# Writes of the routed rows moved from SyncE's DMA queue to ScalarE's, with four buffers in place of two

## The reference

```
scores  = sigmoid(xf @ router_w.T)                  # 4096 rows, 16 experts
4 experts per row, picked within the 2 best of 4 groups; w = their scores, made to sum to 1
shared  = silu(xf @ shared_gate.T) * (xf @ shared_up.T) @ shared_down.T
routed  = sum over a row's 4 experts e of  w[e] * (silu(xf @ gate[e]) * (xf @ up[e])) @ down[e]
out     = x + shared + routed
```

## Time and profile before

| | |
|---|---|
| time, three runs | 1189.49 us median (1186.09, 1189.49, 1204.87) |
| profiled execution | span 1205.0 us; no time of its own is given beside it |
| busy: TensorE matmul / weight load | 87% / 50% |
| busy: VectorE, ScalarE, GpSimd | 53%, 32%, 37% |
| block stage in the profiled execution | about 556 to 954 us |
| last stage | about 954 to 1205 us |

### The profile page before, as it was taken

How to read it: one execution, slowest core, us unless ns; L and a number is a source line. 1 busy time by engine, 2 the same in 40 slices (tenths; PEclk the granted TensorE clock), 3 DMA queues, 4 the chain that set the end, 5 groups by cost and what they waited for, 6 DMA issues and landing times.

```text
span 1205.0 us, 22651 instructions
## 1 busy us (share of the span) xinstructions
PE 1046.4 (87%) x6496; PEld 603.5 (50%) x6497; DVE 638.2 (53%) x1454; ACT 386.1 (32%) x751; POOL 444.0 (37%) x517
## 2 busy tenths in 40 slices
PE   7899499899999988886789999889899877878597
PEld 6576344444444433434566676666666533323243
DVE  4935567533434877995333444434344246547455
ACT  2423243232323544441334443434344301111011
POOL 1730320111100424225334444344444286846650
PEclk9988789999999999997999999999999998989899
DMA  9605763563329315215999999989899686897750
GB/s 348 238 19 179 191 227 106 160 181 113 139 79 222 136 53 184 78 53 128 269 262 244 255 259 260 233 236 227 235 245 255 208 260 198 200 239 238 252 176 35
DMA packets 219262, 229.57 MB, mean 191 GB/s; under 512 B 143670, under 2 KB 152664, under 8 KB 218712
## 3 DMA queue, kind: packets, MB, share of 16 engines
q1 hardware_dynamic: 195676, 151.53, 44.1%
q0 software_dynamic: 23552, 77.61, 22.9%
HBM read 124.99 MB, written 70.55 MB: 162 GB/s over the span
## 4 chain that ended last, share of the span: by engine, by line
PE 44%; DVE 16%; issue 14%; DMA 13%; ACT 4%; another core or an unknown queue 4%; POOL 2%; SPq 1%; DVEq 1%; ACTq 0%; POOLq 0%
PE bank L750 13%; PE bank L900 11%; DMA arena<-arena 6%; PE bank L766 5%; PE bank L919 5%; DVE arena L1516 3%; DMA arena<-xr_dram,arena 2%; PE bank L731 2%; PE bank L885 2%; DVE arena L1274 2%; DVE arena L1450 1%; DMA y_dram<-arena 1%; DMA arena<-xr_dram 1%; PE bank L607 1%
## 5 line engine op out<-in xcount | busy, mean ns | idle before, releaser
L750 PE MATMUL bank<-arena 128*128 (+1 forms) x1536 | 361.3, 394 | 53.9 <-DVE arena L1274 27.3
L750 PEld LDWEIGHTS bank<-arena 128*128 128x128 f16 (+1 forms) x1536 | 154.1, 101 | 252.1 <-issue 65.2
L900 PE MATMUL bank<-arena 128*128 x1728 | 224.5, 278 | 34.0 <-issue 18.6
L900 PEld LDWEIGHTS bank<-arena 128*128 128x128 f16 x1728 | 162.8, 98 | 90.2 <-issue 55.9
L766 PE MATMUL bank<-arena 128*128 128x512 f16 (+1 forms) x768 | 176.2, 380 | 5.5 <-DVE arena L1276 5.5
L1599 POOL DMA_INDIRECT arena<-xr_dram,arena x144 | 141.2, 980 | 55.9 <-issue 43.9
L1629 POOL DMA_INDIRECT arena<-y_dram,arena x128 | 135.2, 1056 | 38.7 <-issue 34.2
L1477 DVE SCALAR_TENSOR_TENSOR arena<-bank,arena 128x128 f32<-128x128 f32 x144 | 41.9, 291 | 178.6 <-ACT arena L1116 140.4
L1053 ACT ACTIVATE arena<-arena 128x512 f16<-128x512 f32 x64 | 40.3, 630 | 262.1 <-DVE arena L1274 235.9
L766 PEld LDWEIGHTS bank<-arena 128*128 128x128 f16 x768 | 74.9, 98 | 96.9 <-DVE arena L1276 6.6
L919 PE MATMUL bank<-arena 128*128 x432 | 117.1, 380 | 0.7
(11 more groups left out here) (173 smaller groups left out, 1130.5 us busy)
## 6 DMA issues: line engine op xcount, KB each, us to landing
y_dram<-arena SPq DMA_DIRECT2D x144, 256.0 KB
arena<-in_x SPq DMA_DIRECT2D x8, 1024.0 KB, 12.4
xr_dram<-arena SPq DMA_DIRECT2D x16, 512.0 KB, 2.9
x_dram<-arena SPq DMA_DIRECT2D x8, 1024.0 KB, 4.7
arena<-x_dram SPq DMA_DIRECT2D x8, 1024.0 KB
arena<-in_gu_w SPq DMA_DIRECT2D x16, 512.0 KB, 3.2
x1s_dram<-arena SPq DMA_DIRECT2D x5, 1024.0 KB, 6.5
arena<-x1s_dram SPq DMA_DIRECT2D x20, 256.0 KB
```

The source lines that it names most:

```text
L750: last = mm(bank[g][:, :], w, xt(xv * KC + kc), start=(n == 0), stop=(n == 3 * KC - 1))
L900: last = mm(bank[2 + j][:, 0:2 * H], rows[:, r // 2, xv * KC + kc, :], only((gu_hi_r, gu_lo_r)[wp], e, slice(kc * 2 * H, (kc + 1) * 2 * H) ...
```

## The change

ScalarE issues the writes of `y_dram` itself. `y_out(s)` comes after the silu of a later block (s+3) and before that block's high half, so about one block later in ScalarE's order than the save_y it belongs to. `y_sb` has four buffers with a semaphore each, the two new ones in space that the shared expert uses in other stages; save_y(s) waits for the write of block s-4. SyncE's loop keeps the transposes. The first four blocks stand ahead of ScalarE's loop. ScalarE waits for the last writes from the two new buffers before it goes on to the shared expert.

```
-        y_sb = view(o3 + 4 * KB, [2, D])
+        y_sb = [view(o3 + 4 * KB, [D]), view(o3 + 6 * KB, [D]), view(o1 + 4 * KB, [D]), view(o1 + 6 * KB, [D])]
...
-        s_yw = [sem("y_written0"), sem("y_written1")]
+        s_yw = [sem(f"y_written{r}") for r in range(4)]
...  (SyncE)
-            def y_out(s, j):
-                sp.wait_ge(s_ye, s + 1)
-                sp.dma_start(item(y_tiles, s), y_sb[:, j, :]).then_inc(s_yw[j], 16)
...
                     turn_odd(h, gathered, sp.to_reg(used) if loop else used)
-                    for r in (2 * h, 2 * h + 1):
-                        y_out(4 * i - 4 + r, r % 2)
...  (ScalarE)
+            def silu_hi(s, j, fresh, out, r):
                 ...
                 A(r_silu[:, j, :], bank[2 + j][:, 0:H], ACT.Silu, scale=1.0 / WS).then_inc(s_rs, 1)
+                if out is not None:
+                    y_out(out, r)
                 act.wait_ge(s_rh, s + 1)
                 ...
+            def save_y(s, r, turn):
                 act.wait_ge(s_rd, s + 1)
+                if not isinstance(turn, int) or turn:
+                    act.wait_ge(s_yw[r], 16 * turn)
+                A(y_sb[r], bank[6 + r % 2][:, :], ACT.Copy, scale=1.0 / WS).then_inc(s_ye, 1)
+
+            def y_out(s, r):
+                act.wait_ge(s_ye, s + 1)
+                act.dma_start(item(y_tiles, s), y_sb[r]).then_inc(s_yw[r], 16)
+
+            def four_blocks(i, first):
                 for n in range(4):
+                    silu_hi(4 * i + 2 + n, n % 2, False, None if first and n == 0 else 4 * i + n - 1, (n + 3) % 4)
+                    save_y(4 * i + n, n, i)
...
+            four_blocks(0, True)
+            with act.Fori(1, BLOCKS // 4 - 1) as i:
+                four_blocks(i, False)
...
+            for r in (2, 3):
+                act.wait_ge(s_yw[r], 16 * BLOCKS // 4)
```

More of the change, by code:

```diff
@@ L562, in _ @@
                 four_blocks(i)
-            for s in range(BLOCKS - 4, BLOCKS):
-                y_out(s, s % 2)
             def take(o, j):
@@ L584, in _ @@
             for j in range(2):
-                sp.wait_ge(s_yw[j], 16 * BLOCKS // 2)
+                sp.wait_ge(s_yw[j], 16 * BLOCKS // 4)
+                sp.wait_ge(s_yw[j + 2], 16 * BLOCKS // 4)
             sp.wait_ge(s_x1sw, 16 * FIRST)
@@ L1110, in _ @@
                         routed_weights_hi((k - WITH) * SPLIT + 2 * i + h, h)
-            def silu_hi(s, j, fresh):
+            def silu_hi(s, j, fresh, out, r):
                 act.wait_ge(s_rg, s + 1)
@@ L1120, in silu_hi @@
                 A(r_hb[:, j, 0, :], r_h[:, j, :], ACT.Copy).then_inc(s_rhh, 1)
-            def save_y(s, j, half):
+            def save_y(s, r, turn):
                 act.wait_ge(s_rd, s + 1)
[L1124 to L1130, removed]
-                for n in range(4):
-                    silu_hi(4 * i + 2 + n, n % 2, False)
-                    save_y(4 * i + n, n % 2, 2 * i + n // 2)
-            for n in range(2):
[L1135 to L1138, removed]
+                if not isinstance(turn, int) or turn:
[5 more added lines that the diff above has]
+            def four_blocks(i, first):
+                for n in range(4):
+                    silu_hi(4 * i + 2 + n, n % 2, False, None if first and n == 0 else 4 * i + n - 1, (n + 3) % 4)
+                    save_y(4 * i + n, n, i)
+            silu_hi(0, 0, True, None, None)
+            silu_hi(1, 1, True, None, None)
+            four_blocks(0, True)
+            with act.Fori(1, BLOCKS // 4 - 1) as i:
+                four_blocks(i, False)
+            for n in range(2):
+                silu_hi(BLOCKS - 2 + n, n, False, BLOCKS - 5 + n, (n + 3) % 4)
+                save_y(BLOCKS - 4 + n, n, BLOCKS // 4 - 1)
+            for n in range(2, 4):
+                y_out(BLOCKS - 5 + n, n - 1)
+                save_y(BLOCKS - 4 + n, n, BLOCKS // 4 - 1)
+            y_out(BLOCKS - 1, 3)
+            for r in (2, 3):
+                act.wait_ge(s_yw[r], 16 * BLOCKS // 4)
             with act.Fori(FIRST, NB) as k:
@@ L1610, in _ @@
                 gather(BLOCKS - 8 + r, r, False, r == 7)
-            for j in range(2):
-                pool.wait_ge(s_yw[j], 16 * BLOCKS // 2)
+            for r in range(4):
+                pool.wait_ge(s_yw[r], 16 * BLOCKS // 4)
             pool.wait_ge(s_rd, BLOCKS)
```

## The result

The changed kernel takes 1207.4 us (median of 12 runs, 1195.9 to 1222.9), the kernel before 1197.4 (12 runs, 1186.1 to 1211.1): ratio 1.010, 95% interval 1.006 to 1.014. It is slower by 1%, small but clear of zero, where 1% faster was forecast. On another chip the same pair gave 1.0117 (1.0037 to 1.0197), on a third 1.0088 (1.0045 to 1.0131).

The account below looks back on a forecast made before the run. In the block stage's second half, transposes issued late, after SyncE's waits for saves, were taken as the bound. 1205.0 - 12 - 1 + 2 = 1194; the same 11 off the median 1189.5 gives 1178 us (1165 to 1186), whole range 1160 to 1202.

Parts of the forecast that it names:

- SyncE's waits for rows: Sign in SyncE's queue: it would wait for gathered rows in most of its 72 transposes.
- the pace of 2.6 after 760 us: Sign in the block stage's second half: blocks at about 2.6 us each, where they took 2.77.
- a shorter wait of GpSimd: Sign at GpSimd's gathers: its wait for transposes would fall well under 115.9 us.
- SyncE's release, -12: Block stage after 760 us: transposes go out when rows land, not after saves; 12 of 15.4 us gained.
- the two regimes: Block stage: DMA engines busy 0.96 to 0.99 up to 760 us; after it 0.85 to 0.94, yet blocks pass more slowly.
- Four buffers, -1: ScalarE's saves: nearly all 44.9 us of waits for writes go, 1 us of it counted as gain.
- ScalarE's issues, +2: ScalarE between silu and high half: 144 issues of 0.41 us, costing 0.05 us at 36 turns, 2 us.
- The first rival: ScalarE's loop turns: issues held by SyncE's transposes cost 1.36 us at each of 36, 1227 us; chance 0.15.
- The transposes lose the writes ahead of them.: SyncE's queue: transposes may start sooner, 1.4 us of a 10.7 us loop, or slow by sharing; no separate term.
- The second rival, the full engines: DMA engines are the bound, so what is issued earlier lands no earlier; 1186 to 1192 us, chance 0.22.
- The first 84 us: Start of the block stage: 27 blocks, no gain taken, as engines are at 0.99 with three 1 MB transfers.
- The middle: Block stage from 640 to 760 us: 47 blocks at 2.55 us each, used as the best pace.

Follow-up runs that it names:

- before_late: The kernel before with the three early 1 MB transfers each four blocks later in SyncE's order: ratio 1.002 (0.998 to 1.006).
- act_tiny2: Against the kernel before: four buffers, SyncE's writes issued two blocks later, and ScalarE issuing a DMA of 256 bytes after each silu: 0.997 (0.993 to 1.001).
- the held kernel: The changed kernel, but SyncE waits for each save as before and then issues a 256-byte DMA in place of the write: 1.0315 to the kernel before.
- ahead_more2: The kernel before with four buffers for odd blocks' gathered rows and 128 KB more written for each block: 1.009 (1.005 to 1.013).
- ahead_sp: The kernel before, writes still on SyncE, with four buffers in place of two for odd blocks' gathered rows: 0.981 (0.973 to 0.989).
- sp_lag: The kernel before with four y_sb buffers and SyncE issuing each write two blocks later: 0.986 (0.978 to 0.994).
- act_pairs: The changed kernel with ScalarE issuing the writes in pairs, at the silus of even blocks: 1.001 (0.997 to 1.006) to the kernel before.

## Why the prediction was wrong

The sum was 1205.0 - 12 - 1 + 2. Of the signs named beforehand, SyncE's waits for rows, ScalarE's near zero for writes and the issues of 0.34 us came true; the pace of 2.6 after 760 us (2.73) and a shorter wait of GpSimd (120.3) did not. Term by term:

- *SyncE's release, -12.* Right in kind and near in size. With the writes in SyncE's own queue it is worth 0.996 to 0.986, 12 us; with ScalarE's, 1.4 to 2.1 points, 17 to 25 us. The view that carried it, 119.5 us of waits for saves against 24.3 for rows, was read rightly, and so was the round of gather and transpose: relaxing it gives 1.9%. That the 12 came out is partly luck: they were 12 of 15.4 us that the blocks after 760 us lost in the one trace there was. The trace of before_late, which is as fast (1.002), has 2.6 us per block after 760 and 45 blocks in 640 to 760, so the two regimes are not a fixed trait of the kernel.
- *Four buffers, -1.* Right in kind, 0.996 with an interval up to 1.001: 0 to 10 us. 44.9 us of ScalarE's waits hid behind other work.
- *ScalarE's issues, +2.* 0.338 us each, for 0.333 from SyncE's row; no cost on the path shows in the trace, the lower bound, since they run beside the silu; act_tiny2 leaves up to 1.1 points open. The first rival (an issue held by SyncE's transpose, 1.36 us at each turn) did not happen: the longest was 0.388 us. The time came out on its side for another reason.
- *"The transposes lose the writes ahead of them."* This step failed. I wrote that no row shows it, gave it no term, and let its two ends (1.4 us off a transpose, or slower by sharing) cancel inside the 12. The move to a second queue is the largest term of all: 2.8%, 34 us, on the wrong side, some 1 point of it from the rhythm of single writes. A transpose and a write are under way together in 11% of 640 to 880 us before and in 29% after, and a transpose takes 4.67 us from issue to last packet, not 3.65. The other traces agree: 3.7 to 3.95 us with all writes in SyncE's queue (4.1 with 20% more bytes), 4.5 to 4.9 with single writes in ScalarE's and SyncE free. An estimate: 0.6 to 1.0 us more in each of 36 rounds of one odd buffer is 22 to 36 us, if every round is on the path. It is not the whole account: the held kernel lost most, at 4.14 us. The range had a bound for ScalarE's issues and none for this.
- *The second rival, the full engines,* was the closest of the stories, with its 1189 of no change, but it too allowed for no gain and never for a loss. It is not shown to be the bound either: the engines moved 288 GB/s in ahead_more2.

  The rule of the Trainium skill cited in the prediction ("DMA: Bandwidth & Descriptors", "Rules for kernel authors") is that spreading DMAs over issuing engines does not help bandwidth. It names no cost; the runs show 2.8%.
- *Both stretches.* The first 84 us: 29 blocks against 27, so not untouched as I had said, in one profile each. The middle, which I had taken as fixed at 2.55, is slower: 2.73, and 44 blocks in another trace of the changed kernel too.

What made the two terms visible was to split the change: neither the result nor the profile after shows a gain of 1 to 2% under a loss of 2.8%. What stays open: why the transposes are slower beside single writes of a second queue. That both are under way together is not enough: in ahead_sp they are in 22% of the time, at 3.94 us per transpose. The engine time per MB does not answer it either, for it does not sort the kernels. Single writes on ScalarE give 1.73 and 1.77, and SyncE's writes 1.51 and 1.52 in the fastest kernels. But before_late, with SyncE's writes and a ratio of 1.002, has 1.70, and half of the writes on ScalarE's queue 1.62 at no cost. Where it fell, the gathers' own rose, from 1.57 to 1.62 in sp_lag and 1.69 in act_pairs: with the total share near 1, the parts trade with each other. Also open are the point that the later 1 MB transfers give, and the share of ScalarE's issuing (at most 1.1 points).

## What to carry to other kernels

When a wait in a shared queue is on the path, free it inside the queue first (issue later, from more buffers): that gave 1.4% here, while the same release by a second queue cost 1%. Where the DMA engines are near full, price a move between queues by its own experiment, and follow one dependent transfer from its issue to its last packet, before and after: 3.65 to 4.67 us told more than the shares of the queues, which mix all transfers. And find the round of dependent transfers that reuses one buffer; twice the buffers in it (1.9%) were worth more than any change of who issues.

## What the hardware showed

- ScalarE issues a 256 KB write in 0.338 us while its own activation is running; 144 of them added no measurable wait (`turn_h` 2.0 us in place of 4.5).
- 256 KB writes, one for each block, in a queue of their own beside SyncE's transposes and GpSimd's gathers cost 2.8% of this kernel (1.0315 / 1.0033); in pairs about 1 point less.
- A 256 KB transpose took 3.65 us from issue to last packet in the kernel before, and 4.67 beside those single writes.
- 140 DMAs of 256 bytes on SyncE's queue cost 0.7 points (0.996 to 1.003) in a stage with nearly full engines; the intervals overlap, so this is not clear of noise.
- A DMA share of 0.98 at 265 GB/s is no ceiling: with 20% more bytes the same engines moved 288 GB/s at a share of 1.04 to 1.07 (a share above 1 is packets of one engine that overlap in the record).
